# Attention in a macaron block: 27 of the 1,152 score banks are exponentiated by VectorE, as a polynomial

## The reference

```python
# x: (2, 2048, 256); 16 heads, d_head 16; L_q, JL_k: 6 numbers of unit length per head and token
attn = jnp.einsum('bqhc,bkhc->bhqk', L_q, JL_k) * 6.0 ** (-0.5)
attn = jnp.where(causal, attn, -jnp.inf)
attn = jax.nn.softmax(attn, axis=-1)
v = (x @ W_v + b_v).reshape(B, T, H, d_head)
out = jnp.einsum('bhqk,bkhd->bqhd', attn, v).reshape(B, T, D)
return out @ W_o + b_o
```

## Time and profile before

| | us |
|---|---|
| median of 3 runs | 1141.98 (1141.83 to 1144.21) |
| profiled execution, its own time | 1139.9 |
| its span | 1137.9 |
| start of the first and of the last exponential | 374.6 and 870.4 |

### The profile page before, as it was taken

One profiled execution on the slowest core, in us unless ns is written; L12 is line 12 of the kernel. 1 busy time (PEld: TensorE's weight loads), 2 busy tenths in 40 slices (PEclk: granted clock), 3 DMA queues, 4 the chain that ended last, 5 costly groups with the idle time before them and its releaser, 6 DMA issues.

```text
span 1137.9 us, 23905 instructions
## 1 busy us (share of the span) xinstructions
PE 1028.8 (90%) x7549; PEld 559.1 (49%) x7549; DVE 664.2 (58%) x1477; ACT 870.4 (76%) x1245; POOL 460.0 (40%) x671
## 2 busy tenths in 40 slices
PE   8998999989887788989899898989899999999995
PEld 4456999946554122222122222222223578999843
DVE  6898788768997422332134345356548686445655
ACT  4226777745887999999999999999998237777710
POOL 1003666457730424331221323431313345677755
PEclk9999999999999899999999999999999999999998
DMA  8911555545766221020201022120100965566655
GB/s 291 276 58 48 172 162 173 155 128 162 223 211 196 73 72 56 11 61 10 66 11 41 30 71 79 29 76 20 48 1 21 282 190 157 166 190 188 182 162 153
DMA packets 125717, 133.80 MB, mean 118 GB/s; under 512 B 13224, under 2 KB 111888, under 8 KB 125616
## 3 DMA queue, kind: packets, MB, share of 16 engines
q1 hardware_dynamic: 109056, 90.95, 25.2%
q0 software_dynamic: 14448, 39.47, 12.9%
q10 hardware_dynamic: 2112, 2.10, 0.6%
HBM read 80.43 MB, written 52.04 MB: 116 GB/s over the span
## 4 chain that ended last, share of the span: by engine, by line
PE 31%; ACT 24%; issue 14%; DVE 8%; POOL 2%; DVEq 1%; DMA 1%; ACTq 0%; POOLq 0%
ACT wide L2077 22%; PE banks L1961 6%; PE banks L2452 6%; PE banks L2377 5%; PE banks L2466 3%; PE banks L1935 2%; PE banks L2386 2%; PE banks L2440 1%; DVE x_res L1632 1%; POOL wide L2083 1%; PE banks L1453 1%; DVE wide L1681 1%; PE banks L1456 1%; PE banks L1975 1%; DVE attn_lines_parts L190 1%
## 5 line engine op out<-in xcount | busy, mean ns | idle before, releaser
L2077 ACT ACTIVATE wide<-banks 128x1536 f32<-128x1536 f32 (+1 forms) x384 | 491.7, 1479 | 5.4 <-PE banks L1935 3.8
L1961 PE MATMUL banks<-wide,attn_attend_v_now 128*32 128x512 f32 (+3 forms) x2560 | 287.7, 540 | 1.7 <-POOL wide L2083 1.6
L2083 POOL TENSOR_SCALAR_AFFINE_SELECT wide<-wide 128x256 f32<-128x256 f32 (+1 forms) x320 | 118.2, 398 | 382.8 <-ACT wide L2077 379.1
L1935 PE MATMUL banks<-attn_attend_q_now,attn_attend_k_now 32*128 32x512 f16 (+3 forms) x1280 | 150.5, 354 | 57.4 <-ACT wide L2077 54.3
L1935 PEld LDWEIGHTS banks<-attn_attend_q_now,attn_attend_k_now 32*128 32x128 f16 x1280 | 38.7, 91 | 291.9 <-ACT wide L2077 246.9
L668 POOL DMA_INDIRECT f_region<-xn_rows,f_token_of x79 | 78.3, 991 | 125.1 <-DVE f_token_of L899 82.4
L2128 DVE COPY sums<-banks 128x512 f32<-128x512 f32 x32 | 22.1, 691 | 163.3 <-PE banks L1961 163.3
L2452 PE MATMUL banks<-f_xnt 128*128 128x128 f32 x752 | 100.5, 277 | 3.8 <-DVE f_more L2678 2.9
L2452 PEld LDWEIGHTS banks<-f_xnt 128*128 128x128 f32 x752 | 91.3, 191 | 6.7 <-issue 5.8
L2565 POOL DMA_INDIRECT last_rows_in<-xn_rows,f_spare x72 | 68.8, 956 | 62.1 <-DVE f_stage L2626 24.4
L1961 PEld LDWEIGHTS banks<-wide,attn_attend_v_now 128*32 128x32 f32 x2560 | 56.3, 108 | 73.7 <-issue 71.8
(11 more groups left out here) (370 smaller groups left out, 1765.2 us busy)
## 6 DMA issues: line engine op xcount, KB each, us to landing
y_half<-f_xnt SPq DMA_DIRECT2D x94, 128.0 KB
y_slots<-wide SPq DMA_DIRECT2D x79, 128.0 KB, 1.7
attn_v<-f_more SPq DMA_DIRECT2D x32, 256.0 KB, 3.0
attn_attend_v_now<-attn_v SPq DMA_DIRECT2D x32, 256.0 KB, 3.2
x_res<-L_attn_x SPq DMA_DIRECT2D x8, 512.0 KB, 7.5
xn_rows<-f_w_all SPq DMA_DIRECT2D x8, 512.0 KB, 5.1
attn_q<-attn_lines_q_out SPq DMA_DIRECT2D x8, 512.0 KB, 3.4
attn_k<-attn_lines_k_out SPq DMA_DIRECT2D x8, 512.0 KB, 4.1
```

The lines of the kernel that those rows point to most:

```text
L1935: last = pe.matmul(score[i % SLOTS][:, j, column:column + columns(u)], k_now[rows, kt * P:(kt + 1) * P], q_now[rows, qc * QW + c0:(qc + 1) ...
L1961: last = pe.matmul(out_bank[qc][rows, c0:QW], v_now[:, kt, rows], probs[:, place, column:column + columns(u)], start=(kt == 0), stop=(u == ...
L2077: act.activation(probs_flat[:, at:at + width_of[i]], score_flat[i % SLOTS][:, 0:width_of[i]], ACT.Exp, scale=SCALE).then_inc(sem.exp_done, 1)
L2083: pool.affine_select(out=part, in_=part, compare_op=ALU.is_ge, fill=0.0, base=0, pattern=[[0, part.shape[1]], [1, P]], channel_multiplier= ...
```

## The change

Twenty-seven banks, each the third bank of a full strip and each of a unit away from the diagonal, leave their strip. The table `RAISED` gives them as pairs (step, strip) for each group: 6 in group 0, 4 in 1, 7 in 2, 4 in 3, 3 in 4, none in 5, 1 in 6, 2 in 7.
- PE leaves the third matmul of the strip out and does it at the end of the pair's earlier step instead (`scores_to_raise`), into `rest_bank`, after waiting for what that bank held.
- ACT's exponential of such a strip is 1024 columns wide, not 1536.
- DVE evaluates the polynomial (`raise_scores`): a copy from PSUM, two `scalar_tensor_tensor` with one operand in PSUM, two with both in SBUF, one `tensor_scalar`, each waiting for the one before it. After the third of the six the PSUM bank is free (`CURVE_SCORES_READ`).
- PE gains waits: `wait_raised` (bank free) ahead of the first value product of a query block, ahead of each projection, each other use of `rest_bank` and each further raised bank; `raised` (polynomial done) ahead of the value products of a unit that needs it.
- The first of the `PROJECT_7` steps moves from 22 to 23, and DVE's additions are placed by a loop over the steps (`between`), half by half, with the polynomials among them.

```diff
-PROJECT_7, PROJECT_6, PROJECT_LATE = (22, 25), (34, 38, 42, 45), (25, 28, 38, 41, 43, 45)
+PROJECT_7, PROJECT_6, PROJECT_LATE = (23, 25), (34, 38, 42, 45), (25, 28, 38, 41, 43, 45)
+RAISED_ONE, RAISED_TWO, RAISED_THREE = (10, 13), (20, 24), (28, 30)
+RAISED_EVEN, RAISED_ODD = ((33, 38), (39, 44), (41, 45), (44, 47)), ((35, 38), (40, 44))
+RAISED = ((RAISED_ONE, RAISED_THREE, *RAISED_EVEN), (RAISED_ONE, RAISED_TWO, *RAISED_ODD),
+          (RAISED_ONE, RAISED_TWO, RAISED_THREE, *RAISED_EVEN), (RAISED_ONE, RAISED_TWO, *RAISED_ODD),
+          (RAISED_ONE, RAISED_TWO, RAISED_THREE), (), (RAISED_THREE,), (RAISED_ONE, RAISED_TWO))
+CURVE_STEPS, CURVE_SCORES_READ = 5, 3
...
+        def wait_raised():
+            if asked[0]:
+                pe.wait_ge(sem.raise_step, CURVE_STEPS * (asked[0] - 1) + CURVE_SCORES_READ)
+        def scores_to_raise(g, i):
...
+            pe.wait_ge(sem.sums_kept, QC * g + sum(i > pv_step[last_of[qc]] for qc in range(QC - 1)))
+            if projected[0]:
+                pe.wait_ge(sem.proj_added, projected[0])
...
+            wait_raised()
+            pe.matmul(rest_bank(i), k_now[rows, kt * P:(kt + 1) * P], q_now[rows, qc * QW:(qc + 1) * QW], start=True, stop=True
+                      ).then_inc(sem.raise_scored, 1)
...
+            if kt == 0:
+                wait_raised()
             pe.wait_ge(sem.exp_done, N * g + last_strip[u] + 1)
+            if raised_before(g, u):
+                pe.wait_ge(sem.raised, raised_before(g, u))
...
+                width = (WIDE - 1) * QW if (g, i) in raised_order else width_of[i]
+                act.activation(probs_flat[:, at:at + width], score_flat[i % SLOTS][:, 0:width], ACT.Exp, scale=SCALE
...
+        def raise_scores(g, i):
...
+            dve.wait_ge(sem.raise_scored, n + 1)
+            done = CURVE_STEPS * n
+            dve.tensor_copy(into, score_of).then_inc(sem.raise_step, 1)
+            dve.wait_ge(sem.raise_step, done + 1)
+            dve.scalar_tensor_tensor(curve[:], into, CURVE_SHIFTS[0], score_of, ALU.add, ALU.mult).then_inc(sem.raise_step, 1)
+            dve.wait_ge(sem.raise_step, done + 2)
+            dve.scalar_tensor_tensor(into, curve[:], CURVE_SHIFTS[1], score_of, ALU.add, ALU.mult).then_inc(sem.raise_step, 1)
+            dve.wait_ge(sem.raise_step, done + 3)
+            dve.scalar_tensor_tensor(into, into, CURVE_SHIFTS[2], curve[:], ALU.add, ALU.mult).then_inc(sem.raise_step, 1)
+            dve.wait_ge(sem.raise_step, done + 4)
+            dve.scalar_tensor_tensor(into, into, CURVE_SHIFTS[3], curve[:], ALU.add, ALU.mult).then_inc(sem.raise_step, 1)
+            dve.wait_ge(sem.raise_step, done + 5)
+            dve.tensor_scalar(into, into, CURVE_LEAD, 1.0, ALU.mult, ALU.add).then_inc(sem.raised, 1)
```

More of the change, by code:

```diff
@@ L1762, in attend @@
     shares = sb("shares", [P, QW // HR])
+    curve = sb("curve", [P, QW])
     sums, below, heads = core.sums, core.below, core.heads
@@ L1821, in attend, with raised_before @@
     assert pv_step[last_of[1]] < 18 and pv_step[last_of[2] + 1] > 25
+    raised_at = [dict(pairs) for pairs in RAISED]
+    raised_order = {(g, strip): n for n, (g, strip) in enumerate((g, strip) for g in range(ALL) for strip in raised_at[g].values())}
+    for strips in raised_at:
+        for i, strip in strips.items():
+            (u, _, _), = score_banks[WIDE * strip + WIDE - 1]
+            assert u not in diagonal and first_column(u) == 0 and pv_step[held_by[strip - RING]] <= i < strip
+    def raised_before(g, u):
+        return max([raised_order[g, strip_of[u, h]] + 1 for h in range(HG) if (g, strip_of[u, h]) in raised_order
+                    and place_of[u, h][0] % WIDE == WIDE - 1] + [0])
     def rested(g, i):
@@ L1923, in tensor @@
     def tensor(pe):
+        asked, projected = [0], [0]
+        def wait_raised():
+            if asked[0]:
+                pe.wait_ge(sem.raise_step, CURVE_STEPS * (asked[0] - 1) + CURVE_SCORES_READ)
+        def scores_to_raise(g, i):
+            strip = raised_at[g][i]
+            (u, h, _), = score_banks[WIDE * strip + WIDE - 1]
+            qc, kt, _ = units[u]
+            rows = slice(h * HR, (h + 1) * HR)
+            pe.wait_ge(q_loaded[qc], 16 * (g + 1))
+            pe.wait_ge(kv_loaded[qc], 32 * (g + 1))
+            pe.wait_ge(sem.sums_kept, QC * g + sum(i > pv_step[last_of[qc]] for qc in range(QC - 1)))
+            if projected[0]:
+                pe.wait_ge(sem.proj_added, projected[0])
+            if rested(g, i):
+                pe.wait_ge(sem.rest_kept, rested(g, i))
+            if g == 0 and i > max(at for _, at in late_at):
+                pe.wait_ge(lines_sem.k_ready, 2 * BLOCKS)
+            wait_raised()
+            pe.matmul(rest_bank(i), k_now[rows, kt * P:(kt + 1) * P], q_now[rows, qc * QW:(qc + 1) * QW], start=True, stop=True
+                      ).then_inc(sem.raise_scored, 1)
+            asked[0] += 1
         def scores(g, i):
@@ L1931, in scores @@
             for j, parts in enumerate(score_banks[WIDE * i:WIDE * (i + 1)]):
+                if j == WIDE - 1 and (g, i) in raised_order:
+                    continue
                 for u, h, column in parts:
@@ L1972, in project @@
                 pe.wait_ge(sem.proj_added, before)
+            wait_raised()
+            projected[0] = before + 1
             for j in range(2):
@@ L2164, in add_up, with between @@
                 bn_stats(dve, core, batch * QC + qc).then_inc(sem.stats_done, 1)
+        def raise_scores(g, i):
+            strip = raised_at[g][i]
+            n = raised_order[g, strip]
+            into, score_of = probs[:, strip % RING * WIDE + WIDE - 1, :], rest_bank(i)
+            dve.wait_ge(sem.pv_done, U * g + held_by[strip - RING] + 1)
+            dve.wait_ge(sem.raise_scored, n + 1)
[11 more added lines that the diff above has]
+            dve.tensor_scalar(into, into, CURVE_LEAD, 1.0, ALU.mult, ALU.add).then_inc(sem.raised, 1)
+        def between(g, first, end, halves, two):
+            for i in range(first, end):
+                if i in halves:
+                    qc, half = halves[i]
+                    add_half(two, qc, half)
+                    if half:
+                        add_up(two, qc)
+                if i in raised_at[g]:
+                    raise_scores(g, i)
         def keep_tiles(n, c):
@@ L2244, in group @@
                     continue
-                if side == 0 and qc == 1 and later(g):
-                    add(two - 1, QC - 1)
+                if qc < QC - 1:
+                    first, end = ((0, 16), (16, 31), (31, N))[qc]
+                    halves = {i: done for i, done in projections(g, side).items() if first <= i < end and (later(g) or side == 1)}
+                    between(g, first, end, halves, two - 1 if side == 0 else two)
                 if g == GATE and qc == 1:
@@ L2249, in group @@
                     routing.statistics(dve, 0, HT)
-                if side == 1 and qc in (1, 2):
-                    for done in ((0,) if qc == 1 else (1, 2)):
-                        add(two, done)
-                        if g == GATE + 3:
-                            dve.wait_ge(sem.stats_done, 3 * QC - 3 + done)
-                            routing.statistics(dve, HT + done * BT, BT)
+                if g == GATE + 3 and qc == 1:
+                    dve.wait_ge(sem.stats_done, 3 * QC - 3)
+                    routing.statistics(dve, HT, BT)
         dve.tensor_reduce(holds[:, 0:1], core.ident[:].rearrange("p (j r) -> p j r", r=HR)[:, :, 0:DH], mybir.AxisListType.XY, ALU.add)
```

7 lines of the change are left out of this document (5 added, 2 removed).

## The result

The changed kernel takes **1154.01 us** (median of 4 runs, 1148.61 to 1156.31) against 1141.9 before: ratio 1.0091, interval 1.0069 to 1.0113. It is slower, above the 1143.1 of the forecast and outside the range that I gave. Run twice more beside the kernel before, it gave 1.0082 (1.0063 to 1.0102) and 1.0052 (1.0034 to 1.0071). The profiled execution took 1148.61, its span 1146.9, 9.0 above the span before.

The account below looks back on a forecast made before the run. ACT was taken to set the end, with PE's reserve thin. Terms -2.1 - 1.1 + 1.0 + 1.8 + 1.5 = +1.1 us on the profiled 1139.9 gave 1141.0, or 1143.1 on the median's scale; range 1138.5 to 1148.

Parts of the forecast that it names:

- The bound: In the attention ACT hardly stops and sets the end; PE's reserve is thin and unevenly spread; shorter strips give 11.4 us at most.
- Step 10: Bank raised at step 10 for strip 13, six times: DVE and PE idle enough, gain 0.35 each, -2.1 us.
- a cushion of 0.3: At strip 16 PE's scores come about 0.3 us early for ACT; a saving of 0.42 uses it up, losing 0.07.
- a rival at 0.15: DVE and POOL hinder each other at the diagonal's last masks, eight places at 0.3: +3.5, 1145.5 us; chance 0.15.
- Steps 20 and 28: Step 20 for strip 24, with the projection moved from 22 to 23: +1.0 us; step 28 for strip 30: -1.1 us.
- The extra matmul: The raised bank's matmul, put elsewhere in PE's order, costs between 0 and 0.32 us; taken as 0.21.
- Groups 1 and 3: Steps 35 and 40: the projection of step 42 waits 0.8 us for its bank; 0.9 each, +1.8 us.
- Groups 0 and 2: Steps 33, 39, 41, 44: three polynomials in a row delay the last unit's products by 0.74; together +1.5 us.
- The polynomial: DVE's six steps per raised bank: five at 0.72 and a sixth at 0.45, 4.05 us in all.
- Group by group: Last strip to last strip: 0 and 2 shorter by about 1, 1 and 3 longer by 1.5 to 2, 5 unchanged, others within 0.3.
- the signs of being wrong: PE waits for no polynomial, a polynomial is outside 3.9 to 4.2 us, or groups 1 and 3 get shorter.

Follow-up runs that it names:

- the later place: Changed kernel with its step 10 banks raised at step 13 for strip 15 instead of strip 13: 1149.84 us, ratio 1.0063 to the kernel before.
- the third set: The changed kernel, unchanged, run a third time beside the kernel before: 1149.81 us, ratio 1.0052.
- twelve places: Changed kernel with only twelve banks raised, at steps 13, 28, 34 and 39, projection back at 22: ratio 0.9957 to the kernel before, then 1137.67 us, 0.9948.

## Why the prediction was wrong, point by point

**The bound** was read rightly: ACT sets the end, PE's reserve is thin and local, and 27 shorter exponentials bring nothing by themselves. Of ACT's busy time only half of the 11 us went, and the trace shows where the rest is: at each stopped strip the stop is 0.11 longer than ACT's idle time there (0.57 with 0.46 idle, 0.95 with 0.84). Elsewhere an exponential's row begins before the last one's ends (1.479 us on average in the earlier trace rows, at a pace of 1.13 to 1.34), and behind a stop a part of it stands alone. The changed kernel has 92 stopped strips and the kernel before 36; 56 times 0.11 is 6 us.

**Step 10, the step that failed.** The forecast had "DVE and PE are idle enough there", a cushion of 0.3 and a gain of 0.35 in each of six places, -2.1. I priced DVE's and PE's idle time there and left POOL out: the term for the wait of the value products on the masks was nothing. The place was +2.0: 4.1 us of error in one term. The mechanism was in the text, as a rival at 0.15, with the right operations and the right rows; but its price was too low. I had 0.3 each in eight places, where the loss is 0.7 in each of the six at step 10 and nothing in the two at step 41: there only a pair of masks grows (1.10 us for 0.65 in group 2), the six behind it take 2.14, and PE waits for none of them. The six masks grow by 1.09 us, not by the 0.6 read from four masks, since three steps run beside them, not two; and they have little slack: in group 2 they would have ended at 515.15 + 2.14 = 517.29, and PE asks for them at about 517.85, so 1.09 us of growth meets 0.55 of slack. The slack was to be read before the run (in group 2 of the kernel before the masks end at 514.51 and PE asks for them at 515.05); the growth could only be scaled up from the four masks. The rule of the Trainium skill, page "SBUF — State Buffer", section "SBUF: two separate sides", says more than I drew from it: whichever side starts first keeps the port pair for its whole instruction. By that rule a DVE step beside a POOL instruction of 2.37 us can be held that long; the trace of the later place agrees (2.74 for 0.69).

**Steps 20 and 28**: 1.9 for the first with its projection, in place of 1.0, and -1.5 for the second, in place of -1.1; together 0.4 for -0.1, since the two errors offset each other. The extra matmul costs what I took: in group 3 at step 40, from the raised matmul to the value products of the next strip, 0.53 us (616.70 to 617.23) where 0.32 is usual, so 0.21.

**Groups 1 and 3**: 0.85 us of waiting for the bank where 0.8 was forecast; 1.0 each in all, for 0.9. **Groups 0 and 2**: waits of 0.83 and 0.69, 0.9 each for 0.74, and "this passes to the end" was right, paid in the next group. The polynomial unhindered is 3.95 us from start to start (556.58 to 560.53), at 0.43 for its sixth step; beside POOL's masks it is 4.2. I had 4.05.

**Group by group** I had said that 0 and 2 get shorter by about 1 and the others stay within 0.3. Group 0 stayed, group 2 grew by 0.25, groups 4 and 7 by 0.6, and groups 1 and 3 grew by 2.6 and 3.2 (0.7 of the latter is the stretch at the lower clock) where I had 1.5 to 2: 0.7 of each miss is step 10, and groups 1 and 3 carry the delay from 0 and 2. Of the signs of being wrong that I gave none came, the polynomial and PE's waits for it being as forecast: none of them watched POOL.

**The rest.** The medians are 1154.0, 1152.6 and 1149.8, that is 12.1, 9.5 and 5.8 above the kernel before; the stops explain 7.2 us of the profile's 9.0. Behind the attention the changed profile is 1.7 us longer. Its exponentials and those of before stand at the same distances, within 0.2 us, for the first 107 us; what comes later varies by that much between executions of before too (266.1 to 267.2), and the changed kernel's three have 267.5 to 267.8. Whether a part of it belongs to the change stays open. So does why the median of its first four runs, 1154.0, stands 5 above its profile when the third set gives 1149.8; the granted clock over a run went from 0.988 (1148.61) to 0.976 (1156.31) there.

## What to carry to other kernels

Before work is given to an idle engine, ask which other engine shares something with it, and whether *that* one's result is waited for at this place: idle time of VectorE beside busy, waited-for GpSimd is not free, and a VectorE step with both operands in SBUF can wait for the whole of a long GpSimd instruction. Where the second operand came from PSUM, the conflict with the masks was gone. And when most places of a change lose, measure each by the stop it makes: twelve places, chosen by the stops and away from POOL's work that is waited for, gave 6.4 us where all twenty-seven cost 6 to 12.

## What the runs showed that was not expected

- Six masks of 128x256 on POOL: 2.14 us beside DVE steps that read or write PSUM, 3.23 beside two steps with two SBUF operands and one `TENSOR_SCALAR`. The DVE steps themselves lose at most 0.08 each there, and 0.16 beside the pair of masks at step 41, but 2 us beside a POOL instruction of 2.37.
- A float32 `TENSOR_SCALAR` of 512 columns takes 0.43 us, where a step with two tensors takes 0.69, and it is held by POOL too (2.42 beside an add).
- Away from the start of group 0 and from stretches at the lower clock, a stop repeats to 0.02 us between executions and chips, even where the whole program differs by 80 us. The attention with twelve banks took 493.1 and 493.2 us in two traces on two such chips.
